# Output staging in four half-slots, and the second expert product moved in the TensorE order, in an attention plus mixture-of-experts layer

## The chip, the cores and the metric

The kernel runs on the 8 cores of one Trainium2 chip. Each core handles 4096 of the 32768 tokens and needs nothing from the others. The metric is the device time of the slowest core, in microseconds (us). The change is compared with the kernel before on that time.

## What is computed

The reference, cut to its core (c = 1024 columns, 16 heads, 8 experts of which 6 are kept per token, attention over every fourth token of a segment of 2048):

```python
xn = layernorm(x)
# attention over tokens 0, 4, 8, ... of each segment of 2048
qkv = xn[:, :, 0::4] @ w_in.T + b_in
o = softmax(causal(q @ k.T / 8)) @ v
attn = zeros; attn[:, :, 0::4] = o @ w_out.T + b_out
# feed-forward, all tokens
shared = silu(xn @ ws1) * (xn @ ws2) @ ws3
w = topk6(softmax(xn @ wr)), normalised to sum 1
h = silu(xn @ w1[e]) * (xn @ w2[e])
routed = sum_e w[e] * (h[e] @ w3[e])
out = x + attn + shared + routed
```

## The kernel before

A core holds two segments (`seg`) of 2048 tokens. The tokens of a segment fall in four groups by residue (`r` = 0 to 3), each of 512 tokens, that is four tiles of 128 tokens (`q`). Group r = 0 is the one that attention is computed for. All weights are kept in SBUF as bf16.

The instructions of each engine are written out in the order in which `em(...)` is called, and each waits on semaphores. So an engine's queue is strictly in order: if one instruction waits, all behind it wait. This holds also for SyncE (SP), which issues the loads of x and the stores of the result, and for GpSimd (POOL), which issues the DMAs that cast or accumulate.

**Layer norm of a tile** (`ln_pre`, lines 303 to 342, and `ln_tr`, lines 344 to 369): SP loads 128 rows of x into one of two `XF` buffers (line 312). VectorE sums them (L315), ScalarE sums the squares (L317), then a chain of small steps goes back and forth between ScalarE (L321, L324, Ln in L331, Exp in L334) and VectorE (L327), and VectorE writes the normalised tile `xn_tm` (L337). TensorE transposes it (L355) and VectorE copies it to `XN` (L364). These steps are mixed in by `ln_pump()`, which emits at most one transposition and one `ln_pre` at each call. A group's tiles can be transposed only when the group before the last has given its `XN` buffer back, which is after its tail.

**A feed-forward group** (`ffn_group`, from line 660):

- the router product (L671, PSUM bank B0), Exp (L679), and small VectorE steps that give the gates `gtm`;
- the shared experts' two products (L721), into banks A0, A1 and then B0, B1;
- the *tail* of the group before this one (below);
- silu of the shared product (L735), the product of the two (L743), and the transposition of the gates (L754, L760);
- the loop over four pairs of experts (`ep` = 0 to 3). TensorE computes xn·W1 of both experts into A0, A1 (L776 with pA), then xn·W2 into B0, B1 (L776 with pB), then two small products that spread the gates over the partitions (L785 into bank Q, L789 into bank K). ScalarE takes silu of A into `s1e` (L793), which frees A. VectorE multiplies it with B into `HP` (L797), which frees B, and multiplies by the gates (L802, L806), which frees Q and K. An `ln_pump()` ends each pair.

**The tail** (lines 814 to 882) is the product with W3 and Ws3, and for r = 0 also with the attention's output weight. For each tile q there are two halves of 512 columns, `Hh` = 0 in bank Q and 1 in bank K: 10 matmuls each (19 for r = 0, L843). ScalarE evicts each half (L860) into its half of a *slot*. There are two slots of 128 x 1024 f32: `osb`, and `WinNat` (a weight staging buffer that is free by then). When both halves are in, GpSimd issues one DMA that adds the rows of x from HBM into the slot (L866, 512 KB). When it has landed, SP issues the store of the slot to `out` (L869, 512 KB). A slot may be written again when its store has landed. The tail of group g is emitted inside group g+1, after the shared products. Two are flushed with nothing behind them on the feed-forward side: after r = 3 of the first segment, before the second attention, and at the very end.

Below, a *group with a layer norm chain* is one in whose expert loop the next group's tiles are normalised: r = 1 and 2 of both segments and r = 3 of the first (in r = 2 of the second only the first pairs have it). For r = 0 the next group's tiles are already done within attention.

Of the kernel before, what the change touches and what calls it, by code (L numbers as in the profile page):

```python
# [8 lines left out]
F32 = mybir.dt.float32  # L9
BF16 = mybir.dt.bfloat16  # L10
AF = mybir.ActivationFunctionType
ALU = mybir.AluOpType
# [3 lines left out]
P = 128  # L16
# [15 lines left out]
def build_nc():  # L32
# [20 lines left out]
    with ctx:  # L53
# [48 lines left out]
        HS = A(nc.sbuf_tensor("HS", [P, 2, 512], BF16))  # L102
        s1e = A(nc.sbuf_tensor("s1e", [P, 2, 512], BF16))
        HP = A(nc.sbuf_tensor("HP", [P, E, 512], BF16))
        out_sb = A(nc.sbuf_tensor("osb", [P, 1024], F32))
        sel = A(nc.sbuf_tensor("sel", [E, E * P], BF16))

        ptT0 = A(nc.psum_tensor("ptT0", [P, CI, P], BF16))
# [551 lines left out]
        def ffn_group(seg, r):  # L660
# [108 lines left out]
            for ep in range(E // 2):  # L769
                e0, e1 = 2 * ep, 2 * ep + 1  # L770

                def mk_w(Wx, bn, e):
                    def f(t):
                        ins = None
                        for ci in range(CI):
                            ins = t.matmul(bview[bn], Wx[:, e, ci, :],  # L776
                                           XN[:, rb, ci, :],
                                           start=(ci == 0), stop=(ci == CI - 1))
                        return ins
                    return f  # L780
                cw10 = em("tensor", mk_w(W1, "A0", e0), waits=wfe + bw("A0"), inc="sp")
                cw11 = em("tensor", mk_w(W1, "A1", e1), waits=wfe + bw("A1"), inc="sp")
                cw20 = em("tensor", mk_w(W2, "B0", e0), waits=wfe + bw("B0"), inc="sp")
                cw21 = em("tensor", mk_w(W2, "B1", e1), waits=wfe + bw("B1"), inc="sp")
                cgb0 = em("tensor", lambda t, e=e0: t.matmul(  # L785
                    pQ[:, :], sel[0:E, P * e:P * (e + 1)],
                    gT[0:E, :, :].rearrange("a b c -> a (b c)"),
                    start=True, stop=True), waits=[("sv", cgt)] + bw("Q"), inc="sp")
                cgb1 = em("tensor", lambda t, e=e1: t.matmul(  # L789
                    pK[:, :], sel[0:E, P * e:P * (e + 1)],  # L790
                    gT[0:E, :, :].rearrange("a b c -> a (b c)"),
                    start=True, stop=True), waits=[("sv", cgt)] + bw("K"), inc="sp")
                cse = em("scalar", lambda s: s.activation(  # L793
                    out=s1e[:, :, :], in_=pA[:, :, :], func=AF.Silu),
                    waits=[("sp", cw10), ("sp", cw11), last_chp2], inc="sa")
                bank["A0"] = bank["A1"] = ("sa", cse)
                cu = em("vector", lambda v, e0=e0: v.tensor_tensor(  # L797
                    HP[:, e0:e0 + 2, :], s1e[:, :, :], pB[:, :, :], op=ALU.mult),
                    waits=[("sa", cse), ("sp", cw20), ("sp", cw21)] +
                          ([state["hp_free"]] if ep == 0 else []), inc="sv")  # L800
                bank["B0"] = bank["B1"] = ("sv", cu)
                chp0 = em("vector", lambda v, e=e0: v.tensor_tensor(  # L802
                    HP[:, e, :], HP[:, e, :], pQ[:, :], op=ALU.mult),
                    waits=[("sv", cu), ("sp", cgb0)], inc="sv")
                bank["Q"] = ("sv", chp0)
                chp1 = em("vector", lambda v, e=e1: v.tensor_tensor(  # L806
                    HP[:, e, :], HP[:, e, :], pK[:, :], op=ALU.mult),
                    waits=[("sp", cgb1)], inc="sv")
                bank["K"] = ("sv", chp1)
                last_chp2 = ("sv", cu)  # L810
                chp_last = chp1
                ln_pump()

            def tail(seg=seg, r=r, chp_last=chp_last, ch=ch):
                fin_last = None
                for q in range(NQ):
                    sl2 = state["fin_slot"] % 2
                    state["fin_slot"] += 1
                    oslot = (out_sb[:, :] if sl2 == 0 else
                             WinNat[:, :, :].rearrange("p a b -> p (a b)").bitcast(F32))  # L820
                    evs = []
                    for Hh in range(2):
                        bn = "Q" if Hh == 0 else "K"

                        def mk_fin(q=q, Hh=Hh, bn=bn, r=r):
                            def f(t):
                                ops = []
                                for k in range(2):
                                    ops.append((HS[:, k, 128 * q:128 * (q + 1)],
                                                Ws3[:, k, 512 * Hh:512 * (Hh + 1)]))  # L830
                                for e in range(E):
                                    ops.append((HP[:, e, 128 * q:128 * (q + 1)],
                                                W3[:, e, 512 * Hh:512 * (Hh + 1)]))
                                if r == 0:
                                    for ci in range(CI):
                                        ops.append((OFM[:, ci, 128 * q:128 * (q + 1)],
                                                    Wo[:, ci, 512 * Hh:512 * (Hh + 1)]))
                                    ops.append((ones1[0:1, 0:P],
                                                brow[0:1, 3 * C + 512 * Hh:
                                                     3 * C + 512 * (Hh + 1)]))  # L840
                                ins = None
                                for i, (lt, rh) in enumerate(ops):
                                    ins = t.matmul(bview[bn], lt, rh,  # L843
                                                   start=(i == 0), stop=(i == len(ops) - 1))
                                return ins
                            return f
                        fw = [("sv", chp_last), ("sv", ch[0]), ("sv", ch[1]),
                              ("swfc", swfc_done)] + bw(bn)
                        if r == 0:
                            fw += [("sv", state["ofm_ready"][seg]), ("sv", wch_ready[31]),  # L850
                                   ("sb", sb_done)]
                        cf = em("tensor", mk_fin(), waits=fw, inc="sp")
                        fin_last = cf
                        ew = [("sp", cf)]
                        if Hh == 0:
                            ew.append(("sst%d" % sl2, 16 * state["st_uses"][sl2]))
                            if sl2 == 1 and state["st_uses"][1] == 0:
                                ew.append(tr_read[0])
                                ew.append(tr_read[1])
                        ce = em("scalar", lambda s, Hh=Hh, bn=bn, oslot=oslot: s.activation(  # L860
                            out=oslot[:, 512 * Hh:512 * (Hh + 1)], in_=bview[bn],
                            func=AF.Identity), waits=ew, inc="sa")
                        bank[bn] = ("sa", ce)
                        evs.append(ce)
                    state["acc_uses"][sl2] += 1
                    em("gpsimd", lambda g, seg=seg, r=r, q=q, sl2=sl2, oslot=oslot: g.dma_start(  # L866
                        out=oslot, in_=xv[seg, r, q], accum_op=ALU.add),
                        waits=[("sa", evs[0]), ("sa", evs[1])], inc="sacc%d" % sl2, k=16)
                    em("sync", lambda sy, seg=seg, r=r, q=q, sl2=sl2, oslot=oslot: sy.dma_start(  # L869
                        out=ov[seg, r, q], in_=oslot),  # L870
                        waits=[("sacc%d" % sl2, 16 * state["acc_uses"][sl2])],
                        inc="sst%d" % sl2, k=16)
                    state["st_uses"][sl2] += 1
                    ln_pump()
                    ln_pump()
                state["hp_free"] = ("sp", fin_last)
                state["hs_free"] = ("sp", fin_last)
                state["gt_free"] = ("sp", fin_last)
                if r == 0:
                    state["ofm_free"] = ("sp", fin_last)  # L880
                state["xnbuf_free"][rb] = ("sp", fin_last)
                ffn_done.add((seg, r))
# [12 lines left out]
        for seg in range(NSEG):  # L895
# [7 lines left out]
        flush_tail()  # L903

        em("sync", lambda sy: sy.nop(),
           waits=[("sst%d" % i, 16 * state["st_uses"][i]) for i in range(2)])

        ninstr = {e: len(sch[e]) for e in ENGS}

# [63 lines left out]
```

How the kernel before makes its waits and increments, by code:

```python
            def run(eng_obj, wt=wt, fn=fn, inc=inc, k=k):  # L139
                for s, v in wt:
                    eng_obj.wait_ge(S[s], v)
                ins = fn(eng_obj)
                if inc is not None:
                    ins.then_inc(S[inc], k)
```

## Time and profile before

| | us |
|---|---|
| median of 2 runs (1016.32 to 1017.26) | 1016.79 |
| the profiled execution, its own time | 1004.06 |
| its span, first to last instruction, slowest core (core 2) | 1002.5 |
| spans of the 8 cores | 993.7 to 1002.5 |
| TensorE matmul busy (73% of the span) | 736.1 |
| ScalarE busy / VectorE busy / GpSimd busy | 285.1 / 265.0 / 68.8 |
| mean granted TensorE clock, share of full speed | 0.862 |

The profile is of the slowest core in one execution. The span leaves out 1.6 us of the execution's own time. The granted clock is the mean of two levels, 1.2 and 2.4 GHz (0.5 and 1.0 of full speed).

Where the time goes by stage, on the profile's clock: weights, the first layer norm and attention 0 to 238 us; first segment's groups 238 to 541 us, with a flush of the last tail to 568 us; second attention 568 to 680 us; second segment's groups 680 to 966 us; last tail to 1002.5 us.

### The profile page before, as it was taken

To read this page: it belongs to the slowest core of one execution; us is meant where nothing else is said; L and a number is where in the kernel's file an instruction comes from. 1 tells how busy PE (TensorE), PEld (TensorE's weight loads), DVE (VectorE), ACT (ScalarE), POOL (GpSimd) and SP (SyncE) were. 2 spreads that over 40 slices of the span, in tenths; PEclk is the share of its full clock that TensorE was granted. 3 is DMA by queue.
4 is the path that set the end of the run, shared out by engine and by line. 5 is a ranking of instruction groups with operands and counts; after the bars stand their busy time and mean duration, and the time that the engine had idled before them with its cause. 6 is when DMAs were issued, how large, how long until landed. Compare 5 with 4: busy or idle time off the path is not lost.

```text
span 1002.5 us, 11868 instructions; the slowest of 8 cores (993.7 to 1002.5 us)
## 1 busy us (share of the span) xinstructions
PE 736.1 (73%) x4126; PEld 337.8 (34%) x4192; DVE 265.0 (26%) x564; ACT 285.1 (28%) x476; POOL 68.8 (7%) x101
## 2 busy tenths in 40 slices
PE   2175656656999687698767878879997787687883
PEld 1132333333443233243323334334443333233331
DVE  2413332332210350152043034123301530330210
ACT  0232312411112450452153155331112622411210
POOL 4101021100001000000000100000000001001000
PEclk9996757766999799899978877978999899788997
DMA  6905474772005303511610620000035106204216
GB/s 102 170 23 89 80 104 57 84 114 43 1 14 122 97 23 82 133 38 22 165 66 4 155 73 23 1 1 1 1 63 147 42 2 146 63 1 96 72 17 152
DMA packets 39624, 67.38 MB, mean 67 GB/s; under 512 B 19856, under 2 KB 21904, under 8 KB 39568
## 3 DMA queue, kind: packets, MB, share of 16 engines
q0 software_dynamic: 30352, 33.06, 23.2%
q1 hardware_dynamic: 9216, 33.56, 10.0%
q8 instruction: 37, 0.61, 0.3%
q14 instruction: 19, 0.16, 0.1%
HBM read 66.11 MB, written 16.78 MB: 83 GB/s over the span
## 4 chain that ended last, share of the span: by engine, by line
PE 53%; DMA 17%; ACT 12%; DVE 8%; issue 8%; POOL 1%; DVEq 0%; ACTq 0%; SPq 0%; POOLq 0%
PE pA L776 8%; PE pQ L843 7%; PE pB L776 7%; PE pK L843 6%; PE pA L427 4%; DMA XF<-x 4%; PE pA L721 4%; DMA osb<-x 3%; DMA out<-osb 3%; PE pA L443 3%; DMA WinNat<-x 3%; PE pB L721 3%; DVE st_s L315 3%; DMA WinNat<-w_in 2%; DVE HP L797 2%
## 5 line engine op out<-in xcount | busy, mean ns | idle before, releaser
L776 PE MATMUL pA<-XN,W 128*128 128x512 bf16 x497 | 125.1, 405 | 61.4 <-ACT s1e L793 48.1
L776 PE MATMUL pB<-XN,W 128*128 128x512 bf16 x501 | 114.5, 379 | 0.6
L776 PEld LDWEIGHTS pA<-XN,W 128*128 128x128 bf16 x512 | 50.5, 103 | 127.8 <-issue 80.9
L211 PE MATMUL ptT<-ident,WinNat 128*128 128x128 bf16 x256 | 30.4, 303 | 64.3 <-DMA WinNat<-w_in 27.8
L843 PE MATMUL pQ<-W,HP 128*128 128x512 bf16 x252 | 72.0, 434 | 0.4 <-issue 0.2
L776 PEld LDWEIGHTS pB<-XN,W 128*128 128x128 bf16 x512 | 50.1, 98 | 60.4
L743 DVE TENSOR_TENSOR HS<-HS,pB 128x512 bf16<-128x512 bf16 x16 | 10.5, 684 | 214.5 <-ACT HS L735 205.8
L797 DVE TENSOR_TENSOR HP<-s1e,pB 128x1024 bf16<-128x1024 bf16 x32 | 39.1, 1221 | 100.8 <-PE pB L776 75.2
L843 PE MATMUL pK<-W,HP 128*128 128x512 bf16 x253 | 60.2, 379 | 0.3
L866 POOL DMA_DIRECT2D osb<-x x16 | 13.5, 844 | 644.4 <-ACT osb L860 644.4
L793 ACT ACTIVATE s1e<-pA 128x1024 bf16<-128x1024 f32 x32 | 32.8, 1024 | 87.0 <-PE pA L776 86.8
L317 ACT ACTIVATE xn_tm<-XF 128x1024 bf16<-128x1024 f32 x32 | 33.7, 1052 | 63.3 <-DMA XF<-x 57.9
L427 PE MATMUL pA<-XN,Wqk 128*128 128x512 bf16 x116 | 42.4, 526 | 11.4 <-DVE Wqk L227 8.6
L315 DVE TENSOR_REDUCE st_s<-XF 128x1 f32<-128x1024 f32 x32 | 38.7, 1210 | 44.3 <-DMA XF<-x 44.3
L843 PE MATMUL pQ<-Ws,HS 128*128 128x512 bf16 x63 | 21.2, 420 | 37.8 <-ACT osb L860 30.0
L211 PEld LDWEIGHTS ptT<-ident,WinNat 128*128 128x128 bf16 x256 | 24.8, 139 | 69.4 <-issue 69.4
L552 DVE TENSOR_TENSOR pT<-pT,utri 128x128 bf16<-128x128 bf16 x128 | 20.2, 219 | 100.7 <-ACT pT L532 98.0
L860 ACT ACTIVATE osb<-pQ 128x512 f32<-128x512 f32 x16 | 9.6, 597 | 129.1 <-PE pQ L843 82.1
L843 PEld LDWEIGHTS pQ<-W,HP 128*128 128x128 bf16 x256 | 27.9, 109 | 39.2 <-issue 15.6
L355 PE MATMUL ptT<-ident,xn_tm 128*128 128x128 bf16 x256 | 24.7, 254 | 21.0 <-DVE xn_tm L337 21.0
L337 DVE TENSOR_SCALAR xn_tm<-XF,st_m,st_r 128x1024 bf16<-128x1024 f32 x32 | 26.2, 819 | 45.6 <-ACT st_r L334 45.6
L721 PE MATMUL pA<-XN,Ws 128*128 128x512 bf16 x120 | 37.0, 472 | 1.0 <-issue 0.5
(138 smaller groups left out, 927.5 us busy)
## 6 DMA issues: line engine op xcount, KB each, us to landing
XF<-x SPq DMA_DIRECT2D x32, 512.0 KB, 4.7
osb<-x POOLq DMA_DIRECT2D x16, 512.0 KB, 5.4
out<-osb SPq DMA_DIRECT2D x16, 512.0 KB, 2.7
WinNat<-x POOLq DMA_DIRECT2D x16, 512.0 KB, 5.4
out<-WinNat SPq DMA_DIRECT2D x16, 512.0 KB, 2.9
WinNat<-w_in POOLq DMA_DIRECT2D x24, 256.0 KB, 5.3
W<-w POOLq DMA_DIRECT2D x16, 256.0 KB, 7.2
W<-w POOLq DMA_DIRECT2D x1, 2048.0 KB, 22.0
```

The costliest lines, as they stand in the source:

```text
L211: ins = t.transpose(bview[tb][:, ci, :], WinNat[:, sl, 128 * ci:128 * (ci + 1)], ident[:])
L315: crs = em("vector", lambda v, seg=seg, j=j, gslot=gslot: v.reduce_sum(st_s[:, seg, j:j + 1], XF[:, gslot, :], axis=AX), waits=ldw, inc="sv")
L317: csq = em("scalar", lambda s, seg=seg, j=j, gslot=gslot, xsl=xsl: s.activation(out=xn_tm[:, xsl, :], in_=XF[:, gslot, :], func=AF.Square, ...
L337: cxn = em("vector", lambda v, seg=seg, j=j, gslot=gslot, xsl=xsl: v.tensor_scalar(out=xn_tm[:, xsl, :], in0=XF[:, gslot, :], scalar1=st_m ...
L355: ins = t.transpose(bview[tb][:, ci, :], xn_tm[:, xsl, 128 * ci:128 * (ci + 1)], ident[:])
L427: t.matmul(pA[:, 0, :], Wqk[:, ci, 128 * hp:128 * (hp + 1)], XN[:, 0, ci, :], start=(ci == 0), stop=False)
L443: t.matmul(pA[:, 1, :], Wqk[:, ci, 1024 + 128 * hp:1024 + 128 * (hp + 1)], XN[:, 0, ci, :], start=(ci == 0), stop=False)
L721: ins = t.matmul(bview[bn], Wsx[:, ci, 128 * k:128 * (k + 1)], XN[:, rb, ci, :], start=(ci == 0), stop=(ci == CI - 1))
L776: ins = t.matmul(bview[bn], Wx[:, e, ci, :], XN[:, rb, ci, :], start=(ci == 0), stop=(ci == CI - 1))
L793: cse = em("scalar", lambda s: s.activation(out=s1e[:, :, :], in_=pA[:, :, :], func=AF.Silu), waits=[("sp", cw10), ("sp", cw11), last_chp2 ...
L797: cu = em("vector", lambda v, e0=e0: v.tensor_tensor(HP[:, e0:e0 + 2, :], s1e[:, :, :], pB[:, :, :], op=ALU.mult), waits=[("sa", cse), ("s ...
L843: ins = t.matmul(bview[bn], lt, rh, start=(i == 0), stop=(i == len(ops) - 1))
```

## The change

There are two parts.

1. **Staging.** The two slots of 1024 columns become four half-slots of 512 columns (`osb` 0 and 1, `WinNat` 0 and 1). Each half is evicted, accumulated and stored by itself: twice as many DMAs, each of 256 KB, with rows of 2 KB instead of 4 KB in HBM. One of the two `ln_pump()` calls per tile in the tail is gone.
2. **Expert loop.** The two gate products (L785, L789) now stand between W1 and W2. And in the last pair (`ep` = 3) the W2 product goes into banks A0, A1 instead of B0, B1, so it waits until silu (L793) has read A.

```diff
+                w2pair = ("B0", "B1") if ep < 3 else ("A0", "A1")
+                w2view = pB if ep < 3 else pA
                 cw10 = em("tensor", mk_w(W1, "A0", e0), waits=wfe + bw("A0"), inc="sp")
                 cw11 = em("tensor", mk_w(W1, "A1", e1), waits=wfe + bw("A1"), inc="sp")
-                cw20 = em("tensor", mk_w(W2, "B0", e0), waits=wfe + bw("B0"), inc="sp")
-                cw21 = em("tensor", mk_w(W2, "B1", e1), waits=wfe + bw("B1"), inc="sp")
                 cgb0 = em("tensor", lambda t, e=e0: t.matmul(
...
                 bank["A0"] = bank["A1"] = ("sa", cse)
+                cw20 = em("tensor", mk_w(W2, w2pair[0], e0), waits=wfe + bw(w2pair[0]),
+                          inc="sp")
...
+                cu = em("vector", lambda v, e0=e0, w2view=w2view: v.tensor_tensor(
+                    HP[:, e0:e0 + 2, :], s1e[:, :, :], w2view[:, :, :], op=ALU.mult),
...
+                bank[w2pair[0]] = bank[w2pair[1]] = ("sv", cu)
...
-                    sl2 = state["fin_slot"] % 2
...
+                        sl4 = state["fin_slot"] % 4
+                        state["fin_slot"] += 1
+                        dst = (out_sb[:, sl4, :] if sl4 < 2
+                               else WinNat[:, sl4 - 2, :].bitcast(F32))
+                        ew = [("sp", cf), ("sst%d" % sl4, 16 * state["st_uses"][sl4])]
...
+                        em("gpsimd", lambda g, seg=seg, r=r, q=q, Hh=Hh, dst=dst: g.dma_start(
+                            out=dst,
+                            in_=xv[seg, r, q][:, 512 * Hh:512 * (Hh + 1)],
+                            accum_op=ALU.add),
+                            waits=[("sa", ce)], inc="sacc%d" % sl4, k=16)
+                        em("sync", lambda sy, seg=seg, r=r, q=q, Hh=Hh, dst=dst: sy.dma_start(
+                            out=ov[seg, r, q][:, 512 * Hh:512 * (Hh + 1)],
+                            in_=dst),
...
-                    ln_pump()
                     ln_pump()
```

How instructions move. On TensorE (`W` stands for both W1 and W2), the last two pairs of experts and the next group's router, before:

```order
L776 MATMUL pA<-XN,W 128x512 x16
L776 MATMUL pB<-XN,W 128x512 x16
L785 MATMUL pQ<-gT,sel 128x512
L789 MATMUL pK<-gT,sel 128x512
L776 MATMUL pA<-XN,W 128x512 x16
L776 MATMUL pB<-XN,W 128x512 x16
L785 MATMUL pQ<-gT,sel 128x512
L789 MATMUL pK<-gT,sel 128x512
L671 MATMUL pB<-Wr,XN 128x8 x32
L721 MATMUL pA<-XN,Ws 128x512 x16
L721 MATMUL pB<-XN,Ws 128x512 x16
```

The same place after the change:

```order
L776 MATMUL pA<-XN,W 128x512 x16
L785 MATMUL pQ<-gT,sel 128x512
L789 MATMUL pK<-gT,sel 128x512
L776 MATMUL pB<-XN,W 128x512 x16
L776 MATMUL pA<-XN,W 128x512 x16
L785 MATMUL pQ<-gT,sel 128x512
L789 MATMUL pK<-gT,sel 128x512
L776 MATMUL pA<-XN,W 128x512 x16
L671 MATMUL pB<-Wr,XN 128x8 x32
L721 MATMUL pA<-XN,Ws 128x512 x16
L721 MATMUL pB<-XN,Ws 128x512 x16
```

The gate products moved ahead of W2 in each pair, and the last pair's W2 is in pA.

On SP, a tail's stores between two sets of x loads, before:

```order
L312 DMA XF<-x 128x1024 x4
L869 DMA out<-osb 128x1024
L869 DMA out<-WinNat 128x1024
L869 DMA out<-osb 128x1024
L869 DMA out<-WinNat 128x1024
L312 DMA XF<-x 128x1024 x4
```

and after the change:

```order
L312 DMA XF<-x 128x1024 x4
L870 DMA out<-osb 128x512 x2
L870 DMA out<-WinNat 128x512 x2
L870 DMA out<-osb 128x512 x2
L870 DMA out<-WinNat 128x512 x2
L312 DMA XF<-x 128x1024 x4
```

The loads of x stand at the same places, behind all stores of a tail. The queues of ScalarE and VectorE keep the order of their instructions too, so the `ln_pump()` that is gone moved nothing.

## Rows read from the trace of the kernel before

**Rows 1.** The page: the chain that ended last, by engine and line.
```profile
PE 53%; DMA 17%; ACT 12%; DVE 8%; issue 8%; POOL 1%; DVEq 0%; ACTq 0%; SPq 0%; POOLq 0%
```
**Rows 2.** Chain of waits, pieces in order: start, length in us, what.
```profile
825.45 0.61 ACT osb L860
...
826.58 5.37 DMA osb<-x
...
832.02 5.40 DMA out<-osb
...
838.25 3.58 PE pQ L843 x10
...
844.50 0.61 ACT WinNat L860
...
845.64 6.42 DMA WinNat<-x
...
852.61 5.88 DMA XF<-x
...
863.84 1.03 ACT s1e L793
```
**Rows 3.** Timeline, TensorE: start, length, operation, idle before it and its releaser.
```profile
865.00 3.57 PE L776 MATMUL pA<-XN,W 128*128 128x512 bf16 x8 [9.70 <-ACT s1e L793]
...
811.89 0.99 PE L671 MATMUL pB<-Wr,XN 128*128 128x8 bf16 x32 [3.60 <-DVE HP L797]
812.74 4.84 PE L721 MATMUL pA<-XN,Ws 128*128 128x512 bf16 x15
817.42 3.62 PE L721 MATMUL pB<-XN,Ws 128*128 128x512 bf16 x16
```
**Rows 4.** Waits: who waited for whom, us in total, times, longest.
```profile
PE pA L776 <- ACT s1e L793: 48.1, 9, 9.7
...
PE pQ L843 <- ACT osb L860: 30.0, 6, 5.8
```
**Rows 5.** Windows: us, busy of PE, PEld, DVE, ACT, POOL, PEclk, DMA share, GB/s.
```profile
820.87:844.34 23.47, 19.16 (x81) 8.03 (x80) 0.00 (x0) 4.08 (x7) 2.54 (x3) 0.93 0.50 112
904.73:929.83 25.10, 19.47 (x80) 8.12 (x80) 0.00 (x0) 4.07 (x7) 2.57 (x3) 0.86 0.50 105
...
541.39:568.30 26.91, 22.46 (x81) 9.07 (x84) 0.00 (x0) 4.33 (x8) 2.54 (x3) 0.80 0.45 98
287.27:321.65 34.38, 34.12 (x152) 14.10 (x153) 0.00 (x0) 4.18 (x7) 2.58 (x3) 1.00 0.39 91
```
**Rows 6.** DMA issues: target, engine, count, size, median us to landing.
```profile
osb<-x POOLq DMA_DIRECT2D x16, 512.0 KB, 5.4
out<-osb SPq DMA_DIRECT2D x16, 512.0 KB, 2.7
...
W<-w POOLq DMA_DIRECT2D x16, 256.0 KB, 7.2
...
brow<-b_out POOLq DMA_DIRECT2D x1, 2.0 KB, 1.9
```
**Rows 7.** Windows as in rows 5, around one accumulate and one store.
```profile
826.60:831.00 4.40, 4.35 (x21) 1.94 (x20) 0.00 (x0) 1.20 (x2) 0.93 (x2) 1.00 0.67 111
831.00:837.00 6.00, 2.98 (x14) 1.17 (x12) 0.00 (x0) 0.00 (x0) 0.75 (x1) 1.00 0.74 181
```
**Rows 8.** Timeline around the last expert pair of a group with a layer norm chain.
```profile
799.52 1.02 ACT L793 ACTIVATE s1e<-pA 128x1024 bf16<-128x1024 f32 x1
...
807.92 0.37 PE L789 MATMUL pK<-gT,sel 8*128 8x512 bf16 x1
...
809.23 1.02 ACT L793 ACTIVATE s1e<-pA 128x1024 bf16<-128x1024 f32 x1
810.42 1.22 DVE L797 TENSOR_TENSOR HP<-s1e,pB 128x1024 bf16<-128x1024 bf16 x1 [1.59 <-ACT s1e L793]
```
**Rows 9.** Timeline around the two flushed tails.
```profile
537.26 1.02 ACT L793 ACTIVATE s1e<-pA 128x1024 bf16<-128x1024 f32 x1
...
962.45 1.22 DVE L797 TENSOR_TENSOR HP<-s1e,pB 128x1024 bf16<-128x1024 bf16 x1 [4.87 <-PE pB L776]
...
965.75 0.63 PE L843 MATMUL pQ<-Ws,HS 128*128 128x512 bf16 x1 [2.87 <-DVE HP L806]
```

More of the change, by code:

```diff
@@ L104, in build_nc @@
         HP = A(nc.sbuf_tensor("HP", [P, E, 512], BF16))
-        out_sb = A(nc.sbuf_tensor("osb", [P, 1024], F32))
+        out_sb = A(nc.sbuf_tensor("osb", [P, 2, 512], F32))
         sel = A(nc.sbuf_tensor("sel", [E, E * P], BF16))
@@ L796, in ffn_group @@
                 bank["A0"] = bank["A1"] = ("sa", cse)
-                cu = em("vector", lambda v, e0=e0: v.tensor_tensor(
-                    HP[:, e0:e0 + 2, :], s1e[:, :, :], pB[:, :, :], op=ALU.mult),
+                cw20 = em("tensor", mk_w(W2, w2pair[0], e0), waits=wfe + bw(w2pair[0]),
+                          inc="sp")
+                cw21 = em("tensor", mk_w(W2, w2pair[1], e1), waits=wfe + bw(w2pair[1]),
+                          inc="sp")
+                cu = em("vector", lambda v, e0=e0, w2view=w2view: v.tensor_tensor(
+                    HP[:, e0:e0 + 2, :], s1e[:, :, :], w2view[:, :, :], op=ALU.mult),
                     waits=[("sa", cse), ("sp", cw20), ("sp", cw21)] +
                           ([state["hp_free"]] if ep == 0 else []), inc="sv")
-                bank["B0"] = bank["B1"] = ("sv", cu)
+                bank[w2pair[0]] = bank[w2pair[1]] = ("sv", cu)
                 chp0 = em("vector", lambda v, e=e0: v.tensor_tensor(
@@ L816, in tail @@
                 for q in range(NQ):
-                    sl2 = state["fin_slot"] % 2
[L818 to L821, printed above, removed]
                     for Hh in range(2):
@@ L853, in tail @@
                         fin_last = cf
[L854 to L862, printed above, removed]
@@ L863, in tail @@
-                        bank[bn] = ("sa", ce)
[L864 to L872, printed above, removed]
@@ L873, in tail @@
-                    state["st_uses"][sl2] += 1
-                    ln_pump()
+                        sl4 = state["fin_slot"] % 4
[3 more added lines that the diff above has]
+                        ew = [("sp", cf), ("sst%d" % sl4, 16 * state["st_uses"][sl4])]
+                        if sl4 >= 2 and state["st_uses"][sl4] == 0:
+                            ew.append(tr_read[sl4 - 2])
@@ new lines, in tail @@
+                        ce = em("scalar", lambda s, dst=dst, bn=bn: s.activation(
+                            out=dst, in_=bview[bn], func=AF.Identity),
+                            waits=ew, inc="sa")
+                        bank[bn] = ("sa", ce)
+                        state["acc_uses"][sl4] += 1
+                        em("gpsimd", lambda g, seg=seg, r=r, q=q, Hh=Hh, dst=dst: g.dma_start(
[3 more added lines that the diff above has]
+                            waits=[("sa", ce)], inc="sacc%d" % sl4, k=16)
@@ L875, in tail @@
+                        em("sync", lambda sy, seg=seg, r=r, q=q, Hh=Hh, dst=dst: sy.dma_start(
+                            out=ov[seg, r, q][:, 512 * Hh:512 * (Hh + 1)],
+                            in_=dst),
+                            waits=[("sacc%d" % sl4, 16 * state["acc_uses"][sl4])],
+                            inc="sst%d" % sl4, k=16)
+                        state["st_uses"][sl4] += 1
                     ln_pump()
@@ L905, in build_nc @@
         em("sync", lambda sy: sy.nop(),
-           waits=[("sst%d" % i, 16 * state["st_uses"][i]) for i in range(2)])
+           waits=[("sst%d" % i, 16 * state["st_uses"][i]) for i in range(4)])
         ninstr = {e: len(sch[e]) for e in ENGS}
```

## The prediction

> **What bounds the kernel now.** The chain that ended last comes first. Only 53% of it is TensorE; DMA has 17%, ScalarE 12%, VectorE 8% [rows 1]. So the kernel is neither TensorE-bound nor DMA-bound throughout: it alternates. The chain in order of time tells where. Take the tail that begins at 820.87 us. The second half of tile 0 is evicted at 825.45, its accumulate takes 5.37 us, its store 5.40 us, and only then can tile 2 be evicted and TensorE begin tile 3 at 838.25. Later the last slot's accumulate (6.42 us) holds up the load of x (5.88 us), because SP's queue is in order and the loads stand behind the last store. That load feeds the layer norm steps, which stand in ScalarE's queue ahead of silu (863.84) [rows 2]. TensorE then resumes with W1 of the second pair at 865.00 after 9.70 us of idle [rows 3]. Waits of the first kind come to 30.0 us over six places, 5.8 the longest, of the second to 48.1 us over nine [rows 4]. So in a tail the reader is to see two waits with one cause, the round trip of a slot: one inside the tail and one a few us later.
>
> The size of the first is read from windows over the tails. A half of a tile takes 10 matmuls and 2.16 us at full clock, so eight take 17.3 us. The tails took 23.47, 25.10 and 26.91 us, at a mean clock of 0.93, 0.86 and 0.80. The tail of r = 0, with 19 matmuls per half, took 34.38 us at full clock, with almost no idle: 34.12 us busy [rows 5]. It leaves the DMAs enough time.
>
> **The change, part by part.**
>
> *Price of a half.* An accumulate of 512 KB lands 5.4 us after issue, a store alone after 2.7 us, a 2 KB DMA of GpSimd after 1.9 us [rows 6]. The trace has no accumulate of 256 KB. Its bounds are 1.9 us and 5.4 us. I take 1.9 plus half of the rest, 3.7 us, since most of the 5.4 grows with bytes: in the 4.4 us after an issue the 16 DMA engines were busy 67%, that is 2.95 us of all of them. In the next 6.0 us, at 74% (4.4 us), one accumulate and one store were served, so a store costs about 1.5 us [rows 7]. A tile thus costs 2.95 + 1.5 = 4.45 us of the DMA engines, against 4.3 us of TensorE. Rows of 2 KB may cost more. The weights with 512-byte rows (1024 rows, 64 to an engine) took 7.2 us; less the 1.9 of the small DMA, 5.3 / 64 = 83 ns each; the accumulates (8 rows of 4 KB to an engine) 3.5 / 8 = 438 ns [rows 6]. On the line through these a 2 KB row costs 235 ns, so two cost 7% more than one of 4 KB. A half-slot then costs 1.07 x 2.2 = 2.4 us of the DMA engines, 2.7 us at the 90% that they may reach. That is more than TensorE's 2.16 us, but four half-slots soften it: walking the eight halves through, the first reuse of a slot comes just in time and the last is 1.2 us late. This is what is late next.
>
> The Trainium skill, in "DMA: Bandwidth & Descriptors", section "Anatomy of one DMA — SWDGE (gpsimd) path", gives a fixed 2.0 us plus bytes at 436 GB/s, and speaks against splitting. By it 512 KB would take 3.2 us and 256 KB 2.6, and a halved accumulate would bring 0.6 us instead of 1.7. The trace disagrees about the part that grows: 5.4 us, not 3.2 [rows 6]. By the page the r = 0 item below would be 1.2 us instead of 3.4.
>
> *Gains in the tails.*
> - Three tails with x loads behind them (r = 1 of the first segment, inside r = 2; the next one; and the one of rows 2). After: TensorE ends at 820.87 + 17.3 + 1.2 = 839.4, eviction and issue take it to 840.5, and the last half's accumulate, behind stores still in flight, lands at about 846, where 852.06 (845.64 + 6.42) was before [rows 2]. All behind it moves as one: 6.0 us each, 18.0. TensorE's own gain in the tail (4.9 us) is swallowed, since it waits for silu anyway: its 9.70 us of idle become 9.70 - 6.0 + 4.9 = 8.6.
> - The tail inside the last group (904.73), with no x load behind it: 25.1 - 18.5 = 6.6 us [rows 5].
> - The flush at 541.39: it starts at the low clock (ten matmuls after an idle stretch took 3.58 us in rows 2; at this tail's lower mean clock I take 2.2 us extra), as before, so 26.9 - (17.3 + 2.2 + 1.2) = 6.2 us.
> - The last tail, 965.75 to 1002.5 = 36.75 us [rows 9]. After: 3.6 for the first half at the low clock, 15.1 for seven more, 1.2 late, 1.2 for eviction and issue, 4.2 accumulate, 2.3 store = 27.6. Gain 9.1.
> - The two tails of r = 0: only the last accumulate shortens, 5.4 to 3.7: 1.7 each, 3.4.
>
> Sum 43.3 us.
>
> *Cost of the last pair's W2 in bank A.* It now waits for silu. Where a layer norm chain runs, silu (ep) to silu (ep + 1) takes 9.7 us (799.52 to 809.23), more than TensorE's work. Before, W2 and the gate products were done at 808.3, silu ended at 810.26, the multiplication at 811.65, and the router began at 811.89 [rows 3, 8]. After, W2 begins at 810.4. TensorE has idled 5.6 us by then instead of 3.6 and will begin at the low clock. After 3.60 us of idle 16 matmuls took 4.84 us, not 3.45 [rows 3]; I take 5.1, to 815.5. The router follows at once, but the shared product waits for the multiplication in bank A: 815.5 + 1.5 = 817.0. It then runs at full clock, 3.45 us, to 820.4, where it ended at 817.4 before [rows 3]. That is 3.0 us; the same place in the two other such groups comes to 2.5, as their shared product lost more to the clock. I take 2.7 x 3 = 8.1. At the flush all of W2 shows: silu ends at 538.3, W2 takes 5.1, the multiplication and gates 3.3, so 546.6 instead of 541.4 [rows 5, 9]: 5.2. In r = 2 of the second segment, where the chain has run out, 1.4. In the last group W2 waits 1.3 us for silu at full clock: 1.4. In the two r = 0 groups 0.2 each. Sum 16.5 us. Behind the waiting W2 are the router and shared products; VectorE and ScalarE have nothing else to do there.
>
> *The gate products ahead of W2* cost nothing: two take 0.5 us, the multiplication starts that much later, and silu is later still: it ended 2 us after the gate products of the pair in a chain group [rows 8]. Were that cover gone it would be 0.5 us in each of 24 pairs, 11 us. Banks Q and K are free, as the last multiplication by gates ends before W1 does. Bound from the other side: nothing. SP and GpSimd issue twice as many DMAs; each still has its 2.16 us per half.
>
> Net: -43.3 + 16.5 = -26.8, say 27 us. The profiled execution took 1004.06 us: 977 after. The median of the runs is 12.7 us above it, so I take the same difference from it: 1016.8 - 27 = 990 us, 2.7% faster.
>
> **The rivals.**
>
> *A: the halves ride for free.* No late slot, and the last accumulate lands 8 us earlier: 3 x 2 + 3 x 1.2 more, and the clock does not fall at W2 (4 less): 27 + 13.6 = 41, 976 us. For: in rows 7 the engines are 26 to 33% idle. Against: TensorE's pace asks more than they gave.
>
> *B: the halves cost two thirds of a whole.* The gain falls to about 26 us and the W2 wait takes 16: 1007 us, no change that can be told. For: accumulates of 6.42 us beside those of 5.37 [rows 2]. Against: the row estimate of 7%.
>
> *C: slower, because the accumulates come to cost by the DMA and not by the byte.* Place: GpSimd's queue in the tails. If each half took what a whole takes, eight would need 8 x 4.45 = 35.6 us of the DMA engines per tail against 17.8 now, the last accumulate would land at 858 instead of 852, and the sum over the tails would turn from -43 to +28. The gain is linear in between: from 54% of a whole (-43) to 100% (+28), so it meets the 16.5 us of W2 at 71%. At 85% the sum is +21 us, 1038 us. It decides from 71% on. Against: the 512-byte rows, which bound a fixed price per row.
>
> *D: the staging change does not reach the chain,* as the x load is late for another reason. Then only the tails' own stalls without x loads go: 6.6 + 6.2 + 9.1 - 16.5 = 5.4 us, 1011 us. Against: the load is issued 0.5 us after the last accumulate lands [rows 2].
>
> **How the numbers follow.** Forecast 0.57, A 0.14, B 0.16, C 0.05, D 0.08. The forecast's own spread is 8 us for the DMA times, 5 for the W2 wait, 5 for the median against the profiled run: 978 to 1002. The range that holds 8 in 10 reaches to A and past B and leaves C: 974 to 1008 us. A measurement of this kernel tells about 2% (20 us) from no change, so faster means below 996.5: 0.48 of the forecast's 0.57 and A, 0.62; B, D and the forecast's rest without C's lower half, 0.34; slower 0.04.
>
> **What would show it right or wrong.** Right: accumulates of 256 KB land in 3.5 to 4.5 us; TensorE's waits for an eviction in a tail, up to 5.8 us before, are under 1.5; the x loads behind a tail are issued 6 us sooner after the tail's start, while the idle for silu shrinks only by about 1 us, as TensorE is early too; the last pair's W2 is a new group in pA, idle 5 to 6 us before it in three groups, and the router's wait is gone. Wrong: a half's accumulate above 4.5 us, DMA share near 0.9 through the tails with TensorE waiting for stores, or the x load no earlier.

## The result, and the profile after

The changed kernel takes 995.3 us (median of 11 runs, 992.2 the fastest), the kernel before, measured again beside it, 1013.5 us (10 runs). The ratio is 0.983, with a 95% interval of 0.979 to 0.988: 1.7% faster, where 2.7% was forecast. The time lies in the stated range (974 to 1008 us). Runs in which one half of the cores showed a lower granted clock are left out of all ratios (here one of each kernel, 1057.0 and 1058.1 us; further down also the second run of experiment 9, 937.5 us). The profiled execution took 993.9 us (1004.06 before), with a span of 992.4 us on the slowest core, 10.1 us less than before.

The page of the changed kernel: the chain that ended last, by engine and by line, which answers to [rows 1].

```profile
PE 54%; DMA 16%; ACT 12%; DVE 9%; issue 7%; POOL 1%; DVEq 0%; ACTq 0%; SPq 0%; POOLq 0%
PE pA L776 11%; PE pK L842 6%; PE pQ L842 6%; DMA WinNat<-x 5%; PE pB L776 5%; PE pA L427 5%; PE pA L721 3%; DMA XF<-x 3%; PE pA L443 3%; PE pB L721 3%; DVE st_s L315 3%; DMA WinNat<-w_in 2%; DVE HP L801 2%; ACT s1e L793 2%; PE ptT L211 2%
```

The kind of bound is the same as before: the chain still alternates between TensorE and DMA. The waits of the changed kernel (us in total, times, longest), which answer to [rows 4]:

```profile
PE pA L776 <- ACT s1e L793: 64.6, 17, 8.9
...
ACT osb L860 <- DMA out<-osb: 33.8, 11, 4.8
...
PE pK L842 <- ACT osb L860: 6.1, 5, 2.0
```

TensorE's wait for an eviction, 30.0 us before with 5.8 the longest, has come down to 6.1 us with 2.0 the longest. The waits for a free slot are still there (33.8 us for `osb`, where the kernel before had 47.0), but mostly only ScalarE stands in them. The wait for silu has grown from 48.1 us in 9 places to 64.6 in 17: the new ones are those of the last pair's W2.

The chain of waits of the changed kernel through the same tail as in [rows 2] (it now begins at 824.64 us):

```profile
833.59 0.61 ACT WinNat L860
...
834.73 5.60 DMA WinNat<-x
...
840.39 5.39 DMA out<-WinNat
...
845.86 0.61 ACT WinNat L860
...
846.99 5.30 DMA WinNat<-x
...
852.85 4.45 DMA XF<-x
...
862.64 1.03 ACT s1e L793
...
863.81 6.21 PE pA L776 x15
```

The shape is that of before, with half the bytes in each DMA: accumulate, store, eviction, accumulate, x load, silu. Only the matmuls that stood behind the eviction (838.25 in [rows 2]) are no longer in the chain. But the accumulates of half the size still take 5.30 and 5.60 us, and the store 5.39. From the eviction into a half-slot to the next eviction into it 12.27 us pass (833.59 to 845.86). The whole slot of [rows 2] took 12.05 us, from 825.45 to the next eviction, in the same chain of the kernel before:

```profile
837.50 0.61 ACT osb L860
```

In this tail the round trip of a slot did not become shorter. What the half-slots gain is that it starts a half earlier, since an accumulate no longer waits until both halves of a tile are in.

The DMA issues of the changed kernel, against [rows 6]:

```profile
osb<-x POOLq DMA_DIRECT2D x32, 256.0 KB, 4.6
out<-osb SPq DMA_DIRECT2D x32, 256.0 KB, 4.4
WinNat<-x POOLq DMA_DIRECT2D x32, 256.0 KB, 5.5
out<-WinNat SPq DMA_DIRECT2D x32, 256.0 KB, 3.1
```

The stores of half the size did not land sooner either: 4.4 and 3.1 us, where a whole one from `osb` took 2.7 (median of all; 5.40 in the tail of [rows 2]). Landing times are not the engines' own time, though. The queue of GpSimd's DMAs on the two pages (packets, MB, share of the 16 engines' span), before and after:

```profile
q0 software_dynamic: 30352, 33.06, 23.2%
```

```profile
q0 software_dynamic: 34960, 33.06, 24.3%
```

That is 232.6 us of the 16 engines (0.232 x 1002.5) and 241.2 us (0.243 x 992.4) for the same bytes. The queue carries the weights too, which did not change, so splitting 32 accumulates cost 8.6 us in all, 0.27 us for a tile. The engines' time went by the bytes; the time until a half has landed did not.

Windows over three tails, columns as in [rows 5]:

```profile
824.64:843.57 18.93, 17.66 (x81) 7.60 (x80) 0.00 (x0) 4.18 (x7) 5.93 (x7) 1.00 0.63 126
904.77:924.26 19.49, 17.52 (x82) 7.67 (x80) 0.00 (x0) 4.18 (x7) 5.08 (x6) 1.00 0.59 123
...
289.82:324.28 34.46, 34.46 (x154) 14.17 (x152) 0.00 (x0) 4.18 (x7) 5.98 (x7) 1.00 0.44 91
```

The two tails took 23.47 and 25.10 us before, at a clock of 0.93 and 0.86. Now they take 18.93 and 19.49 at full clock, with TensorE busy for 17.66 and 17.52 of them: most of the stall is gone and the clock does not fall.

One core of each kernel is a thin base for differences of a few us, so the stages were measured on all eight: in each core's timeline, the start of the router, of the tail, of the gate transposition (L754, the end of a tail), and of the second pair's W1 (the first matmul behind the wait for silu). Medians over the 8 cores, in us. "Staging" and "expert" are the runs with one part of the change alone, told below.

| stage (groups as segment.r) | before | after | staging | expert |
|---|---|---|---|---|
| 0.0: second W1 to router + router to tail | 31.5 | 32.1 | 31.5 | 32.1 |
| tail of 0.0 | 34.5 | 34.5 | 34.5 | 34.5 |
| 0.1: tail's end to second W1 | 19.4 | 17.9 | 18.0 | 19.1 |
| 0.1: second W1 to router | 30.4 | 34.8 | 30.6 | 34.8 |
| 0.1: router to tail | 9.4 | 8.7 | 9.5 | 8.7 |
| tail of 0.1, in 0.2 | 24.6 | 18.5 | 18.3 | 24.5 |
| 0.2: tail's end to second W1 | 18.6 | 20.4 | 21.7 | 19.0 |
| 0.3: second W1 to flushed tail | 31.9 | 38.0 | 31.9 | 37.9 |
| flushed tail and second attention | 137.5 | 129.6 | 131.5 | 135.2 |
| tail of 1.2, in 1.3 | 24.7 | 18.6 | 18.8 | 24.8 |
| 1.3: tail's end to second W1 | 10.4 | 12.9 | 12.9 | 10.4 |
| 1.3: second W1 to last tail | 25.2 | 26.7 | 25.2 | 26.7 |
| last tail to the end | 36.3 | 30.3 | 31.5 | 34.8 |
| sum over all stages, these and the others | 996.8 | 983.7 | 972.1 | 1017.7 |

### The profile page after: what moved, and what is told of

It reads as the page before. It is cut to its first block, busy times and chain, and to the rows that moved or that the text cites. A ratio compares the mean times of both kernels' runs of the same rounds, so it can differ in the third digit from the quotient of the medians.

```text
span 992.4 us, 12080 instructions; the slowest of 8 cores (981.8 to 992.4 us)
## 1 busy us (share of the span) xinstructions
PE 745.5 (75%) x4192; PEld 337.2 (34%) x4192; DVE 264.6 (27%) x564; ACT 285.9 (29%) x476; POOL 96.0 (10%) x133
## 3 DMA queue, kind: packets, MB, share of 16 engines
q1 hardware_dynamic: 13824, 33.56, 10.1%
## 4 chain that ended last, share of the span: by engine, by line
PE 54%; DMA 16%; ACT 12%; DVE 9%; issue 7%; POOL 1%; DVEq 0%; ACTq 0%; SPq 0%; POOLq 0%
PE pA L776 11%; PE pK L842 6%; PE pQ L842 6%; DMA WinNat<-x 5%; PE pB L776 5%; PE pA L427 5%; PE pA L721 3%; DMA XF<-x 3%; PE pA L443 3%; PE pB L721 3%; DVE st_s L315 3%; DMA WinNat<-w_in 2%; DVE HP L801 2%; ACT s1e L793 2%; PE ptT L211 2%
## 5 line engine op out<-in xcount | busy, mean ns | idle before, releaser
L776 PE MATMUL pA<-XN,W 128*128 128x512 bf16 x640 | 172.6, 431 | 79.2 <-ACT s1e L793 64.6
L776 PEld LDWEIGHTS pA<-XN,W 128*128 128x128 bf16 x640 | 67.2, 108 | 175.3 <-issue 122.9
L865 POOL DMA_DIRECT2D osb<-x x32 | 27.2, 850 | 638.0 <-ACT osb L860 635.0
L776 PE MATMUL pB<-XN,W 128*128 128x512 bf16 x384 | 87.0, 380 | 0.0
L211 PE MATMUL ptT<-ident,WinNat 128*128 128x128 bf16 x256 | 30.4, 302 | 65.4 <-DMA WinNat<-w_in 27.4
L842 PE MATMUL pQ<-W,HP 128*128 128x512 bf16 x256 | 61.6, 384 | 0.0
L793 ACT ACTIVATE s1e<-pA 128x1024 bf16<-128x1024 f32 x32 | 32.8, 1024 | 89.2 <-PE pA L776 89.0
L427 PE MATMUL pA<-XN,Wqk 128*128 128x512 bf16 x128 | 46.6, 530 | 8.0 <-DVE Wqk L227 6.9
L776 PEld LDWEIGHTS pB<-XN,W 128*128 128x128 bf16 x384 | 35.6, 98 | 49.8 <-issue 10.2
L801 DVE TENSOR_TENSOR HP<-s1e,pB 128x1024 bf16<-128x1024 bf16 x24 | 29.3, 1221 | 79.9 <-PE pB L776 64.0
L211 PEld LDWEIGHTS ptT<-ident,WinNat 128*128 128x128 bf16 x256 | 24.8, 137 | 70.5 <-issue 70.5
L842 PEld LDWEIGHTS pQ<-W,HP 128*128 128x128 bf16 x256 | 25.4, 99 | 31.3 <-issue 2.0
L842 PEld LDWEIGHTS pK<-W,HP 128*128 128x128 bf16 x256 | 25.0, 98 | 30.2
```

Of the source, the lines that this page charges most:

```text
L211: ins = t.transpose(bview[tb][:, ci, :], WinNat[:, sl, 128 * ci:128 * (ci + 1)], ident[:])
L427: t.matmul(pA[:, 0, :], Wqk[:, ci, 128 * hp:128 * (hp + 1)], XN[:, 0, ci, :], start=(ci == 0), stop=False)
L776: ins = t.matmul(bview[bn], Wx[:, e, ci, :], XN[:, rb, ci, :], start=(ci == 0), stop=(ci == CI - 1))
L793: cse = em("scalar", lambda s: s.activation(out=s1e[:, :, :], in_=pA[:, :, :], func=AF.Silu), waits=[("sp", cw10), ("sp", cw11), last_chp2 ...
L801: cu = em("vector", lambda v, e0=e0, w2view=w2view: v.tensor_tensor(HP[:, e0:e0 + 2, :], s1e[:, :, :], w2view[:, :, :], op=ALU.mult), wait ...
L842: ins = t.matmul(bview[bn], lt, rh, start=(i == 0), stop=(i == len(ops) - 1))
```

## The experiments

Each is compared with the kernel before in runs on the same chip. The median of the runs of before that count moved between sets (1009.3 to 1014.8 us), so the ratios are what counts.

**1. The staging part alone.** The edit is the second half of the diff above (four half-slots) and none of its first half.

> The change's staging part alone (four half-slots), experts as before. Theory P (the two parts add, and each is what the stage table of the two profiles says): the tails and what follows them give 35 us, so 979 of 1013.5 us, ratio 0.966; the expert loop keeps its old stage times (ep1 to router 30.5 us in groups with a layer norm chain), and the tails of ten matmuls per half take 18.6 us as in the changed kernel. Rival Q (the gain in the tails is small by itself, and the expert part pays nothing): ratio 0.983, as the whole change.

Measured: 980.6 us (4 runs), ratio 0.969 (0.964 to 0.975). Theory P holds, Q falls: without the expert part the same staging brings 3.1%. The stage table shows where. It also shows that in the tails it behaves as in the changed kernel, 18.3 to 19.1 us.

**2. The expert part alone.** The first half of the diff, with the old staging.

> The change's expert part alone (gate products ahead of W2, last pair's W2 in bank A), staging as before. Theory P: slower by 20 us, ratio 1.020: 3.6 us in each of three groups with a layer norm chain, 6.1 at the flush, 1.5 in the last group, little elsewhere; W2 of the last pair waits 5.5 us for silu in the groups with a chain. Rival Q: the wait for silu is absorbed by the router that no longer waits: ratio 1.000 within 0.005.

Measured: ratio 1.020 (1.010 to 1.030), 2% slower. 0.969 x 1.020 = 0.988, against 0.983 (0.979 to 0.988) for both: the parts add, within their intervals. The stage sums, one execution each, are a coarser measure: they give 24.7 us gained and 20.9 lost, 3.8 together, against 13.1 for the whole change. So the sums can be off by several us; some 6 of these 9.3 us lie ahead of the first router and in the stretches from a router on. The stages that grow are those expected: 30.4 to 34.8 us, 31.9 to 37.9, 25.2 to 26.7.

**3. Only the gate products ahead of W2.**

```diff
-                w2pair = ("B0", "B1") if ep < 3 else ("A0", "A1")
-                w2view = pB if ep < 3 else pA
+                w2pair = ("B0", "B1")
+                w2view = pB
```

> Only the gate products moved ahead of W2; all W2 in bank B, staging as before. Theory P: nothing, ratio 1.000 within 0.004, since silu ends later than W2 in the groups with a chain. Rival R (the moved gate products carry the loss of the expert part, 0.5 us in each pair of the chain that binds): up to 11 us, ratio 1.011.

Measured: ratio 1.006 (1.003 to 1.009), between the two: theory P's bound of 1.004 is passed, though the interval touches it. In the groups with a layer norm chain it costs nothing (30.4 and 30.8 us in that stage, 30.4 and 30.6 before). In the three groups without one (0.0, 1.0 and 1.3) the stage grows by 0.63 us: there silu is not late, the multiplication follows W2 directly, and W2 now ends later. That is 1.9 us, or 0.002. The rest of the 0.006 shows in no stage of the expert loops, and stays open; of the stage sum's 4.3 us, 2.6 lie ahead of the first router, where the two kernels are the same.

**4. Only the bank of the last W2.** Gate products behind W2 as before.

```diff
+                if ep == 3:
+                    cw20 = em("tensor", mk_w(W2, "A0", e0), waits=wfe + bw("A0"), inc="sp")
+                    cw21 = em("tensor", mk_w(W2, "A1", e1), waits=wfe + bw("A1"), inc="sp")
```

> Only the last pair's W2 in bank A (behind silu); the gate products stay behind W2 in all pairs, so in the last pair they too come after the wait. Staging as before. Theory P (the bank carries the loss): slower by 14 to 19 us, ratio 1.014 to 1.019, the two parts of the expert change adding up to 1.020. Rival R (the gate products in front carry a large part of it, 0.5 us in every pair): ratio below 1.010.

Measured: ratio 1.018 (1.015 to 1.022). Theory P holds. In the chain groups the last pair's W2 waits 5.5 to 5.7 us for silu (medians over the 8 cores). The loss of the expert part is the wait of W2 behind silu.

**5. The price of an accumulate by its shape.**

```diff
+                    pq = [slice(0, 128), slice(0, 128), slice(0, 64), slice(0, 128)][q]
+                    cq_ = [slice(0, 1024), slice(0, 512), slice(0, 1024), slice(0, 256)][q]
...
-                        out=oslot, in_=xv[seg, r, q], accum_op=ALU.add),
+                        out=oslot[pq, cq_], in_=xv[seg, r, q][pq, cq_], accum_op=ALU.add),
```

> The kernel before, but the accumulate of tile q has another shape: q = 0 all 128 x 1024, q = 1 128 x 512, q = 2 64 rows x 1024, q = 3 128 x 256; the rest of x is left out of the sum. Read in the tails of r = 0, where the DMAs do not overlap. Theory B (price by bytes, as the prediction took it): 5.4, 3.7, 3.7 and 2.8 us to landing. Theory R (price by the number of rows that an engine handles one after another): 5.4, 4.2 to 4.9, 3.6 and about 4 us, so that 64 long rows land sooner than 128 short ones of the same bytes.

The DMA issues of this kernel, one row for each shape, in the order 128 x 1024, 128 x 512, 64 x 1024, 128 x 256 (median us to landing last):

```profile
osb<-x POOLq DMA_DIRECT2D x8, 512.0 KB, 6.5
WinNat<-x POOLq DMA_DIRECT2D x8, 256.0 KB, 4.2
osb<-x POOLq DMA_DIRECT2D x8, 256.0 KB, 4.3
WinNat<-x POOLq DMA_DIRECT2D x8, 128.0 KB, 3.0
```

Both theories lose a part. 128 rows of 2 KB and 64 rows of 4 KB cost the same, 4.2 and 4.3 us, so the number of rows is not the price: theory R is out. But it is not straight in the bytes either. Those rows are of one core, over all tails. In the two r = 0 tails, where one accumulate follows the other by 8.6 us and none is in flight with another, the medians over the 8 cores are 5.6 us for 512 KB (5.3 to 6.6; the core of these rows had 6.5 there too, and why is not known), 4.2 and 4.4 for the two shapes of 256 KB, 3.1 for 128 KB. Halving 512 KB saves 1.4 us, not 1.7. The prediction's straight line from 1.9 us at 2 KB to 5.4 us at 512 KB would give 2.8 and 3.7 us where 3.1 and 4.2 were measured: it lies too low in the middle.

**6. Early loads of x, in the kernel before.** A helper issues each load of x as soon as the tile that frees its buffer has been emitted. In SP's queue the loads then stand ahead of a tail's stores.

```diff
-            em("sync", lambda sy, seg=seg, r=r, q=q, gslot=gslot:
-               sy.dma_start(out=XF[:, gslot, :], in_=xv[seg, r, q]),
-               waits=state["xf_free"][gslot], inc=sxn, k=16)
+            if state["tile"] == 1:
+                xload(0)
+                xload(1)
...
             state["xf_free"][gslot] = [("sv", cxn), ("sa", csq)]
+            xload(seg * NT + j + 2)
```

> The kernel before; only each load of x is put in SP's queue right behind the tile that frees its buffer, so that it stands ahead of a tail's stores. Theory S (after a tail silu waits for the x load, and the load waits for nothing but the stores ahead of it in SP's queue): gate transposition to W1 of the second pair falls from 18.6 to 19.4 us to about 11.3 in five groups, 38 us, ratio 0.962. The waits inside the tails stay. Rival T (the load would be late anyway, since the DMA engines are busy with the accumulates, or the layer norm steps in front of silu take the time): less than 12 us, ratio above 0.988.

Measured: 969.6 us, ratio 0.959 (0.955 to 0.963). Theory S holds. The stage from a tail's end to the second W1 is 11.4 us in all five groups (18.6 to 19.4 before), and the tails keep their 24 to 25 us. So the load of x was late for the stores ahead of it in SP's queue: put ahead of them, it leaves that stage at the same 11.4 us in every group.

**7. Early loads with the half-slots, and 8. with the whole change.** The same edit on the kernel of experiment 1 and on the changed kernel.

> Four half-slots (the change's staging part alone) with the early loads of x. Theory S: both add, since the one shortens the tails (24.5 to 18.6 us) and the other what follows them (18.0 to 21.7 us down to 11.3): 979 - 41 = 938 of 1013.5 us, ratio 0.927. Rival T: ratio above 0.957.

> The changed kernel with the early loads of x. Theory S: the cost of W2 in bank A does not depend on when x arrives, since it comes from the chain of layer norm steps between one silu and the next: the last pair's W2 still waits 5.5 us, and the ratio is 0.927 + 0.017 = 0.945. Rival U (the chain in the expert loop is late only because the x loads start late, and its lateness goes with them): the wait before W2 falls under 2 us and the ratio comes within 0.005 of the early loads with staging alone.

Measured: 940.1 us, ratio 0.930 (0.928 to 0.933), and 958.9 us, ratio 0.949 (0.946 to 0.952). Both near what theory S has (0.927 and 0.945), and far from T and U. Experiment 7 is the fastest kernel of this study that computes the whole result, 7.0% faster than before and 5.4% faster than the change (0.930 / 0.983). The stage behind the tails is 11.4 to 13.3 us in both. The last pair's W2 keeps its wait, here in the timeline of TensorE in experiment 8:

```profile
780.60 4.85 PE L785 MATMUL pA<-XN,W 128*128 128x512 bf16 x11 [5.49 <-ACT s1e L802]
```

5.49 us, to the digit that of the changed kernel (below), though x came several us sooner: rival U falls. The lateness of silu in the last pair is the length of the chain of layer norm steps from one silu to the next. That is 9.63 us both here and at the place of [rows 3] in the changed kernel, whatever the x load does:

```profile
769.80 1.02 ACT L802 ACTIVATE s1e<-pA 128x1024 bf16<-128x1024 f32 x1
...
779.43 1.02 ACT L802 ACTIVATE s1e<-pA 128x1024 bf16<-128x1024 f32 x1
```

```profile
799.45 1.02 ACT L793 ACTIVATE s1e<-pA 128x1024 bf16<-128x1024 f32 x1
...
809.08 1.02 ACT L793 ACTIVATE s1e<-pA 128x1024 bf16<-128x1024 f32 x1
```

**9. Half-slots without accumulates.** x is not added to the output, and the store waits for the eviction alone.

```diff
-                        em("gpsimd", lambda g, seg=seg, r=r, q=q, Hh=Hh, dst=dst: g.dma_start(
...
-                            waits=[("sacc%d" % sl4, 16 * state["acc_uses"][sl4])],
+                            waits=[("sa", ce)],
```

> Four half-slots with no accumulate at all: x is not added, each store waits for the eviction alone. Theory V (what the prediction mis-sized is the price of a half's accumulate, and it is what the half-slot version still waits for): no wait for an eviction in a tail, so all tails take 17.3 us (18.3 to 19.1 with accumulates), the x load is issued within 2 us of the tail's end, and gate transposition to W1 of the second pair takes 13 us where it took 18.0 to 21.7; the last tail ends 6 us sooner; about 945 us together. Rival W (SP's issue or the stores themselves set the pace): tails of 18 us or more, and that stretch stays above 16 us.

Measured: 925.6 us. The experts are as before, so the stages are compared with experiment 1, the same kernel with its accumulates. The four tails of ten matmuls per half that lie inside a group took 17.36 us each, the time of TensorE alone; the five stretches behind tails took 12.0 to 13.7 us, the last tail 22.2 us instead of 31.5. Theory V holds and W falls: what the half-slot version still waits for is the accumulate, its own time and what it does to the stores beside it; the two are not told apart. The time is below the 945 us forecast, since the last tail gained 9.3 us and not 6, and the five stretches behind tails 5.6 to 8.1 us each.

## Why the prediction was right, and where its sizes were off

The mechanism was right in both parts: experiments 1 to 4 show a gain in the tails and a loss in the last pair, and that they add within the intervals. The net came out at 13.1 us by the sum of the stages (1.3%) and 1.7% by the ratio, against 27 us. Gains were forecast too large and the loss too small.

That the 990 us were missed by only 5.3 is in part luck. The profiled execution was forecast at 977 us and took 993.9. The 12.7 us between it and the median, which the prediction carried over, were 1.4 us in the changed kernel, and the kernel before came out 3.3 us lower when measured again.

Of the prediction's own signs, these came true: the new wait of W2 (5.49 us), no wait of the router for the multiplication, and an idle for silu behind the three tails that shrank only a little (medians over the 8 cores 7.7, 8.0 and 8.0 us before, 6.5, 6.8 and 7.8 after). TensorE's longest wait for an eviction was 2.0 us, not under 1.5. And one sign of being wrong came up: a half's accumulate was to land in 3.5 to 4.5 us, above 4.5 was to count against the prediction, and the medians are 4.6 and 5.5. The two others of that kind did not: the DMA share in the tails is 0.63 and 0.59, and the x load is earlier.

Term by term, from the stage table (before to after):

- **Price of a half.** Forecast 3.7 us; measured 4.2 alone (experiment 5) and 4.6 and 5.5 as medians over the tails. This is the mis-sized term. Alone it is 0.5 us above the midpoint that was taken, and the rest comes with other DMAs in flight. In the tail of [rows 2], after the change, the eight accumulates took 4.21, 4.92, 5.81, 5.60, 4.82, 5.25, 6.38 and 5.30 us from issue to landing: only the first, with nothing beside it, is as fast as alone. The engines' own time, 7% more for rows of 2 KB by the prediction, was about right: 0.27 us more on the 4.45 of a tile. The x load was to be issued 6.0 us sooner after the tail's start. Over the 8 cores it was issued 32.5, 31.9 and 32.3 us after it before (medians for the three tails) and 27.5, 27.2 and 27.5 after, 4.7 to 5.0 us sooner, and the stages moved by as much (4.3, 4.9 and 5.1), as forecast. In the one tail shown above it is less, 3.5 us (852.61 less 820.87, against 852.85 less 824.64). The three tails gave 14.3 us instead of 18.0, the last tail 6.0 instead of 9.1.
- **The tails themselves.** Eight halves were to take 18.5 us; they took 18.5 to 18.9. Right.
- **The tail in the last group.** Forecast 6.6 us, measured 6.1 in the tail, of which 2.6 us were given back right behind it (10.4 to 12.9 us). This is a wait that the prediction did not follow: TensorE runs ahead of ScalarE now, and the last half's eviction waits for its slot with silu of the shared product queued behind it. The timeline of the changed kernel at the end of the tail of [rows 2], where it is plainest, with what each waited for:

```profile
845.86 0.60 ACT L860 ACTIVATE WinNat<-pK 128x512 f32<-128x512 f32 x1 [3.76 <-DMA out<-WinNat]
846.47 1.28 ACT L735 ACT_TABLE_LOAD   x1
...
847.77 1.08 ACT L735 ACTIVATE HS<-pA 128x512 bf16<-128x512 f32 x2
848.51 5.30 PE L776 MATMUL pA<-XN,W 128*128 128x512 bf16 x16 [4.00 <-ACT HS L735]
```

  4.00 us of idle, where 2.09 were before, and W1 at the low clock behind it. With an x load behind the tail this costs nothing, as TensorE waits for that anyway. In the last group it does: over the 8 cores the median idle there went from 2.43 to 3.31 us, and the 16 matmuls of W1 from 3.45 to 5.15 us, 2.6 us together.
- **The flush.** Forecast 6.2 us, measured 7.9 with the attention behind it. Of this and of the last tail's 6.0 us the staging alone gives 6.1 and 4.9. The expert part alone shortens the same two stages by 2.3 and 1.5 us, which the prediction did not have; so a part of the gain in the flushed tails belongs to the other half of the change. **The tails of r = 0.** Forecast 1.7 us each, measured 1.5 and 1.4.
- **W2 in bank A.** The idle before it was forecast at 5.6 us. The timeline of the changed kernel at the place of [rows 3]:

```profile
810.25 5.90 PE L776 MATMUL pA<-XN,W 128*128 128x512 bf16 x16 [5.49 <-ACT s1e L793]
815.99 0.94 PE L671 MATMUL pB<-Wr,XN 128*128 128x8 bf16 x32
817.74 3.61 PE L721 MATMUL pA<-XN,Ws 128*128 128x512 bf16 x16 [0.81 <-DVE HP L801]
```

  The mechanism is as told: W2 waits 5.49 us, the router follows at once, the shared product waits 0.81 us for the multiplication and runs at full clock. Off is the time of W2 at the low clock: 5.9 us here, 4.9 to 6.6 in the four places, where 5.1 was taken. The chain groups lost 3.6, 3.3 and 3.9 us, 10.9 instead of 8.1, the flush 6.1 instead of 5.2; r = 2 of the second segment lost 0.5 instead of 1.4, the last group 1.5 instead of 1.4, and the two r = 0 groups 0.7 each instead of 0.2.
- **The gate products ahead of W2.** Forecast nothing. Experiment 3 gives a ratio of 1.006: nothing in the chain groups, 0.63 us in each of three others. The cover that was named, a late silu, is absent there.

Together the gains were 34.6 us instead of 43.3 (14.3 + 3.5 + 7.9 + 6.0 + 2.9) and the losses 20.3 instead of 16.5; 1.1 us more was lost before the first router, where nothing was changed. The stages thus give 13.1 us, a little under the 1.7% of the ratio (17 us of 1013.5), whose interval begins at 1.2%.

Of the rivals, B (a dearer half, 10 us in all) came nearest: the ratio's 17 us lie between it and the forecast's 27. By the time to landing a half cost even more than B's two thirds, 0.75 of a whole alone (4.2 of 5.6 us) and more in the tails. On rival C's line, which turns the change into a loss from 71% on, that would have made the kernel slower. It did not, because that line counts the DMA engines' time, and this stayed near half for a half. A fell with the price. C fell with experiment 1. D fell with experiment 6: the chain does run through the accumulates and the x load.

## What to carry to other kernels

Where a queue issues both stores that wait for late results and loads that could go early, look at the order first: moving the x loads ahead of the stores gave 4.1% with a dozen lines and no change of the work, more than the halved staging (3.1%). A product should not be put into the bank that the activation before it still reads unless that activation is on time; here that one choice cost 1.8%, and the staging's gain of 3.1% shrank to 1.7%. And a part of a change that helps can carry one that hurts, so time them apart.

## What the runs showed of the hardware that was not expected

An accumulating DMA issued by GpSimd, with no other in flight, took 3.1 us for 128 KB, 4.2 to 4.4 for 256 KB and 5.6 for 512 KB (medians over the 8 cores in experiment 5), and it made little difference whether 256 KB were 128 rows of 2 KB (4.2) or 64 rows of 4 KB (4.4). In the tail shown, with others in flight, 256 KB took up to 6.38 us, though the 16 DMA engines were busy for only 0.63 of that tail.

After nearly the same idle, TensorE resumed at either clock. With 1.88 us of idle before it, the first pair's W1 in the kernel before took 3.61 us, at a granted clock of 1.00 (first row). With 1.93 us, the same place of the changed kernel took 5.11 us, at 0.70 (second row). Nor is it the 0.05 us: at this place all 8 cores of the changed kernel idled 1.93 us, two of them took some 5.1 us and six some 3.6. What decides between the two was not tried.

```profile
324.39 3.61 PE L776 MATMUL pA<-XN,W 128*128 128x512 bf16 x15 [1.88 <-ACT HS L735]
```

```profile
327.15 5.11 PE L776 MATMUL pA<-XN,W 128*128 128x512 bf16 x16 [1.93 <-ACT HS L735]
```
